# Tying embedding gathers to the ends of gram chunks in a recommendation tower kernel

## What is computed

```
e = jnp.stack([tbl_0[ids[:, 0]], ..., tbl_31[ids[:, 31]]], axis=1)     # 2048 x 32 x 64
gram = jnp.einsum('bnd,bmd->bnm', e, e)
z = gram[:, rows, cols]                                                 # pairs n < m
h = jnp.concatenate([z.reshape(2048, -1), dense_ctx], axis=1)           # 2048 x 512
h = jnp.maximum(h @ W_top1 + b_top1, 0.0)                               # 512 x 512
h = jnp.maximum(h @ W_top2 + b_top2, 0.0)                               # 512 x 256
y = h @ W_top3
```

## Time and profile before

| | us |
|---|---|
| median of 3 runs | 451.77 (450.62 to 455.04) |
| profiled execution, its own time | 454.5 |
| span in its profile | 452.7 |
| PE (TensorE matmuls) busy | 398.1, 88% |
| DVE (VectorE) busy | 230.6, 51% |
| ACT (ScalarE) busy | 166.9, 37% |
| POOL busy | 304.6, 67% |
| mean granted clock of TensorE | 0.981 of full speed |

### The profile page before, as it was taken

One profiled execution on the slowest core, in us unless ns is written; L12 is line 12 of the kernel. 1 busy time (PEld: TensorE's weight loads), 2 busy tenths in 40 slices (PEclk: granted clock), 3 DMA queues, 4 the chain that ended last, 5 costly groups with the idle time before them and its releaser, 6 DMA issues.

```text
span 452.7 us, 15283 instructions
## 1 busy us (share of the span) xinstructions
PE 398.1 (88%) x6516; PEld 223.7 (49%) x6516; DVE 230.6 (51%) x717; ACT 166.9 (37%) x264; POOL 304.6 (67%) x968
## 2 busy tenths in 40 slices
PE   0677778999969998799899999879999999988998
PEld 0343334455546554455445554445554655455476
DVE  2999999745438972007148885003417896000000
ACT  3347665511075423220354444112054434421222
POOL 6888898888848898778558888778608888000000
PEclk9999999999989999899999999897999999999999
DMA  6953912100147931010077621100027511024610
GB/s 169 378 147 93 340 44 63 47 19 19 20 74 138 286 75 24 16 20 17 17 137 163 193 60 44 20 18 18 14 42 156 116 22 22 6 33 77 118 52 0
DMA packets 38238, 37.53 MB, mean 83 GB/s; under 512 B 13781, under 2 KB 26903, under 8 KB 38042
## 3 DMA queue, kind: packets, MB, share of 16 engines
q1 hardware_dynamic: 31594, 29.04, 25.7%
q0 software_dynamic: 6144, 6.30, 6.9%
q10 hardware_dynamic: 432, 1.21, 0.8%
HBM read 28.45 MB, written 8.09 MB: 81 GB/s over the span
## 4 chain that ended last, share of the span: by engine, by line
PE 75%; DVE 14%; issue 6%; ACT 3%; DMA 2%; DVEq 0%
PE sel_ps L500 38%; PE tower_ps L545 13%; PE gram_ps L529 11%; DVE onehot L447 10%; PE tower_ps L555 6%; PE gat_ps L514 3%; PE tower_ps L500 2%; DVE tabs L435 2%; ACT vecs L310 2%; DVE work L430 2%; PE tower_ps L564 2%; DMA ids_wide<-ids_scratch 1%; DMA ids_scratch<-sel_f 1%; DMA sel_ids<-in_ids_sel_dram 1%; ACT tabs L303 0%
## 5 line engine op out<-in xcount | busy, mean ns | idle before, releaser
L447 DVE TENSOR_SCALAR onehot<-ids_wide,row_ids 128x512 bf16<-128x512 f16 x688 | 202.0, 365 | 123.2 <-PE sel_ps L500 76.2
L500 PE MATMUL sel_ps<-onehot,tabs 128*64 128x512 bf16 x1968 | 226.7, 386 | 32.4 <-DVE onehot L447 16.7
L276 POOL DMA_INDIRECT rows<-in_tbl_dram,gat_ids x192 | 195.2, 1016 | 46.8 <-PE sel_ps L500 18.2
L500 PEld LDWEIGHTS sel_ps<-onehot,tabs 128*64 128x64 bf16 x1968 | 118.8, 111 | 135.0 <-issue 39.7
L272 POOL MEMSET spare<- 128x1 f32 x768 | 109.1, 142 | 33.2
L310 ACT COPY vecs<-sel_ps 64x256 f32<-64x256 f32 x152 | 92.1, 606 | 103.1 <-PE sel_ps L500 60.1
L529 PE MATMUL gram_ps<-vecs 64*32 64x32 f32 x4096 | 51.8, 201 | 19.5 <-issue 18.6
L529 PEld LDWEIGHTS gram_ps<-vecs 64*32 64x32 f32 x4096 | 43.3, 105 | 44.7 <-issue 42.0
L545 PE MATMUL tower_ps<-work,w_sb 128*128 128x512 f32 (+1 forms) x160 | 62.8, 539 | 0.0
L545 PEld LDWEIGHTS tower_ps<-work,w_sb 128*128 128x128 f32 x160 | 30.1, 197 | 20.9 <-issue 18.8
L454 DVE COPY work<-gram_ps 128x512 f32<-128x512 f32 x8 | 5.2, 688 | 58.4 <-PE gram_ps L529 58.4
(11 more groups left out here) (16 smaller groups left out, 41.3 us busy)
## 6 DMA issues: line engine op xcount, KB each, us to landing
ids_wide<-ids_scratch SPq DMA_DIRECT2D x40, 256.0 KB
rows<-in_tbl_dram,gat_ids POOLq DMA_INDIRECT x192
products<-work SPq DMA_DIRECT2D x12, 248.0 KB
products<-work SPq DMA_DIRECT2D x24, 120.0 KB
work<-in_packed_dram SPq DMA_DIRECT2D x5, 512.0 KB
work<-products SPq DMA_DIRECT2D x9, 256.0 KB
work<-in_packed_dram SPq DMA_DIRECT2D x3, 640.0 KB
work<-in_packed_dram ACTq DMA_DIRECT2D x2, 512.0 KB
```

Source lines behind the costliest of these rows:

```text
L276: nc.gpsimd.indirect_dma_start(out=rows[:, r, k, h, :], out_offset=None, in_=tables[GATHERED[k]], in_offset=bass.IndirectOffsetOnAxis(ap=g ...
L447: last = nc.vector.tensor_scalar(onehot[:, n % RING, c - c0, :], ids_wide[:, k, :], row_ids[chunks[k]][:, c:c + 1], None, ALU.is_equal)
L500: last[at] = nc.tensor.matmul(sel_bank(u, g)[DIM * at:DIM * at + DIM, :], tabs[:, first_chunk[k] + c, part, :], onehot[:, piece_no(u, g, h ...
```

## The change

The ranges `CLOSE` go. Gathers 48 to 65 keep six spacers, and all others get three. The wait for `onehot_used` stays at gather 66 and goes at 113 and 164. Eighteen gathers listed in `BEHIND` wait for the end of a gram chunk. For that TensorE counts a second semaphore, `gram_half`, at the end of the even chunks, beside `gram_full` at the odd ones.

```diff
-SPACERS, WIDE_SPACERS = 3, 6
-
-CLOSE = [range(0, 48), range(18, 42), range(17, 45), range(20, 48)]
+WIDE_SPACERS, SPACERS = 6, 3
+WIDE_SPACED = range(48, 66)
+
+BEHIND = {91: (1, 0, 0), 93: (1, 0, 1), 95: (1, 0, 2), 97: (1, 0, 3),
+          103: (1, 1, 0), 104: (1, 1, 1), 106: (1, 1, 2), 107: (1, 1, 3),
+          140: (2, 0, 0), 142: (2, 0, 1), 144: (2, 0, 2), 146: (2, 0, 3),
+          152: (2, 1, 0), 153: (2, 1, 1), 155: (2, 1, 2), 156: (2, 1, 3),
+          190: (3, 0, 0), 191: (3, 0, 1)}
...
+            def chunk_done(u, r, c):
+                pool.wait_ge(gram_full if c % 2 == 1 else gram_half, emptied_no(u, r, c // 2) + 1)
+
...
-                    if n > 0 and n == CLOSE[u].start:
-                        pool.wait_ge(onehot_used, piece_no(u, 4 if u == 1 else 2, 0, 1) + 1)
+                    if len(of_unit) * u + n in BEHIND:
+                        chunk_done(*BEHIND[len(of_unit) * u + n])
+                    if len(of_unit) * u + n == WIDE_SPACED.stop:
+                        pool.wait_ge(onehot_used, piece_no(1, 4, 0, 1) + 1)
                     gather(u, r, x, k, h)
-                    for _ in range(SPACERS if n in CLOSE[u] else WIDE_SPACERS):
+                    for _ in range(WIDE_SPACERS if len(of_unit) * u + n in WIDE_SPACED else SPACERS):
                         spacer()
...
-                if c % 2 == 1:
-                    last.then_inc(gram_full, 1)
+                last.then_inc(gram_full if c % 2 == 1 else gram_half, 1)
```

More of the change, by code:

```diff
@@ L143, in dlrm_tower_kernel @@
         gat_emptied = sem("gat_emptied")
+        gram_half = sem("gram_half")
         gram_full = sem("gram_full")
```

## The result

| | before | after |
|---|---|---|
| median, us | 451.76 (450.62 to 455.04, 4 runs) | 432.87 (432.00 to 433.80, 4 runs) |
| ratio | | 0.9564 [0.9502, 0.9626] |
| profiled execution, its own time / span | 454.5 / 452.7 | 432.0 / 430.2 |
| mean granted clock | 0.981 | 0.992 |
| PE busy | 398.1 | 387.4 |

What follows compares the result with a forecast made beforehand. Gathers stopping TensorE's instruction issue in gram chunks, and the clock falls that follow, bound the kernel. Gains 9.5 + 13.9 less 1.1 (supply) and 0.3 (grazing) make 22.0; 454.5 - 22.0 = 432.5 us, range 428.5 to 440.5.

Steps and rivals of the forecast that it cites:

- The stop of 1.3 us per gather in a chunk: Gram chunks: each gather beginning inside one stops TensorE's supply of instructions, costing 1.3 us.
- Units 1 and 2 laid end to end: TensorE's work at undisturbed steps: unit 1 49.36 to 39.87 us, unit 2 58.66 to 44.72; gains 9.5 and 13.9.
- The clock, 6.3 us: Units 1 and 2: three low-clock stretches after two stopped chunks vanish; 6.3 us, contained in the units' gains.
- the 2.7 us between profile and median: Shown median 451.77 lies 2.7 below the profiled execution; one or two fewer low-clock stretches might explain it; forecast left at 432.5.
- The supply, 1.1 us: Gram chunks without gathers beside them: TensorE's instruction supply itself is late next, taking 1.1 us off the gain.
- Grazing, 0.3: Gathers' stops that touch a chunk's head take 0.3 us off the gain, 0.1 of it at unit 3's first chunk.
- The clock came back: Rival denying this: idle time at chunk heads or instruction waits keep three stretches low; 438.8 us, chance 0.10.
- gathers started 0.3 us behind the end of their chunk's row as priced (183.17 to 183.45) and not 1.5: Rival of late release: gathers start 1.5 us after their release, costing about 8 us at some 14 chunks; 440 us, chance 0.10.
- VectorE stretched the trains by nothing that mattered: Rival: VectorE slows gathers, so from 1.73 us each the train reaches chunk (2,0,0); 2.6 us, 435, chance 0.06.
- no block paid for the gather at its head: Slower rival: 18 gathers behind chunks find the queue empty, 1.3 us each, 23.4 in all; 455.9 to 459 us, chance 0.04.

Runs made afterwards that it cites:

- x_gather: Changed kernel plus four extra gathers, one beginning inside each of chunks (2,0,0) to (2,0,3), into an unread buffer; 428.31 us on chip 8, one run.
- before_again: The kernel before, unchanged, run again on chip 5 for a profile of its own; 450.81 us (7 runs).
- unit0_close: Changed kernel with unit 0's chunks also kept clear, one spacer within its gather pairs, two behind gathers 66 to 90; 452.69 us, 1.0011 to the kernel before.
- shift64: Changed kernel with 64 more TensorE instructions (32 weight loads, 32 tiny matmuls) ahead of its first work; 428.77 us on chip 0, one run.
- x_spacers: Changed kernel with six more spacers (memsets) inside each of chunks (2,0,0) to (2,0,3) and no DMA; 426.45 us on chip 8, one run.
- pace_only: Kernel before with the changed kernel's spacers and none of its waits for chunks; 430.82 us on chip 0, ratio 1.0004 to the kernel before.

## Why the prediction was right, and where it was not

**The stop of 1.3 us per gather in a chunk.** Right for the chips of the recorded runs, 5 and 3. The added gather of `x_gather` shows the cause, and `before_again` the size. That it is the supply of instructions that stops, and not the array, is inferred, and two things speak for it. Where a gather starts before a chunk, or at its head, 39 to 45 matmuls still run in the trace of before and then TensorE stops, as if that many were queued behind the large ones; where it starts later, TensorE stops with it (41 in the chunk at 208.46, 45 in the one at 180.84; in the latter the second gather, 2.26 us into the chunk, stops it at once). And in `unit0_close` closely spaced gathers starve TensorE even where matmuls are large. On chips 8 and 0 the same gather costs about 0.45 us, which the prediction had no way to see.

**Units 1 and 2 laid end to end.** 39.87 was predicted for unit 1 and 39.87 came. For unit 2 it was 44.72 against 45.08; the 0.36 over is the stop of the supply in chunk (2, 1, 3).

**The clock, 6.3 us.** The mechanism held in the profile: no low stretch is left in units 1 and 2, and 6.2 us of the 22.5 are the clock's. That two stopped chunks come before a fall is not borne out: the one at 283.9 stands behind a single one, (2, 0, 0). And it is a term of that execution. `before_again` has stops of the same length and no fall there, in 449.46 us. Against that profile the gain is 17.6, against the medians 18.9 and 17.4. The prediction came out at the right time since it subtracted the clock's share from the same execution that paid it, as it said of the 2.7 us between profile and median.

**The supply, 1.1 us.** Mis-sized. The six intervals of 304 instructions in 3.9 us came through without a stop; only the one in (2, 1, 3) is there, 0.4 us instead of 1.1, and that was in the trace of before already (0.41 us). Whether unit 1 has one depends on its place in the stream: with 64 instructions put in front it had one of 1.2 us. By the rule of the Trainium skill (Runtime: NRT & Kernel Launch, section Instruction fetch mechanics) the term would have been 0, which is nearer in units 1 and 2. In unit 3 that rule's hiding fails, by 0.3 to 0.9 us in six of eight chunks, at the places that `shift64` moved.

**Grazing, 0.3.** Nothing was grazed in the recorded profile: the last gather of the train in unit 3 starts 1.3 us before chunk (3, 0, 0). Of these two terms, 1.4 us together, 0.4 came. The 1.0 too much was made up by unit 0, which came out 1.04 us longer than in the profile of before since the clock stayed low longer near 130 us. Nothing was changed there, and on chip 5, where that stretch is 6.8 us long in both kernels, it was 0.3 us shorter in the changed one. That the two cancel is luck. Another 0.5 us came behind unit 2, for which the sum has no term.

**Rivals.** The clock came back, gathers started 0.3 us behind the end of their chunk's row as priced (183.17 to 183.45) and not 1.5, VectorE stretched the trains by nothing that mattered, and no block paid for the gather at its head. A slowdown by gathers did exist, though not where the rival put it. It needed no chunk at all, only two spacers instead of three.

## What to carry to other kernels

Where an engine runs streams of very short instructions, lay POOL's indirect DMAs beside its "issue" idle time: tying them to the end of such a stream cost nothing here, since the work behind it is long. Price a gather by its period too, and not by its place alone: where the period comes near to the stop (1.36 against 1.3 us), the whole engine starves, so the spacing in a row of gathers is not slack until TensorE's rows say so. And take the times on more than one chip, since the edit that gave 4% where it was recorded and on chip 5 gave little on two others: its near copies `x_spacers` and `shift64` took 1.1% and 0.5% less than the kernel before there, in one run each.

## What the runs showed of the hardware

- The kernel before takes 450.8 to 451.8 us at the median where it was recorded and on chips 5 and 3, and 430.9 to 431.1 on chips 0 and 8. The kernel before was not traced on chips 0 and 8, but `pace_only` on chip 0 is near it, and puts the gap into stops: in units 1 and 2 a gather in a chunk costs 1.3 us on the one kind and 0.2 to 0.5 on the other, with a gather's own time the same. Why they differ stays open, and with it whether it is the chip or a state of it; no counter in the profile shows it. The changed kernel itself was not run on a chip of the second kind. Its variant with only some memsets added took 426.45 us there in one run, and 432.9 and 433.4 is what the changed kernel takes on the first kind: the gap between the kinds shrinks from some 20 us to some 6 (some 4 by `shift64`, 428.77 us on chip 0).
- On both kinds a gather stops a running chunk twice, with 3 to 5 matmuls between the stops on the long kind. Where stops are short, they last from the gather's start to 0.2 us and from 0.4 to 0.65, and a gather that starts 0.6 us before a chunk does no harm. Where they are long, they last from its start to 0.6 us and from 0.65 to 1.3, and a start 0.24 us before it costs the chunk 0.7 us.
- A plain DMA issued by POOL inside a chunk (0.59 us) or by SyncE did not stop TensorE on chip 8. Whether the same holds on a chip with long stops was not tried.
- The clock's falls behind stopped chunks differ from run to run at nearly equal stops (10.1 and 8.9 us in units 1 and 2, against 10.3 and 9.2): 13.6 us at 1.2 GHz in units 1 and 2 of the recorded profile, none in `before_again`.
